# Early flag, unit matrix, output bias and last norms on VectorE, weight preparation in pieces, and a new step order in a four-layer graph kernel

## What is computed

```python
x = _layernorm(x + _L0_gnn_ref(x, adj, W, a))      # attention, one head, leaky ReLU
x = _layernorm(x + _L1_gnn_ref(x, adj, ...))       # attention with logits h A h^T, ELU
x = _layernorm(x + _L2_gnn_ref(x, adj, ...))       # 4 heads; relu(out @ Wo + bo)
x = _layernorm(x + _L3_gnn_ref(x, nodemask, adj, ...))
# L3: one gated sum per relation 2..40, and a "loop" relation 1;
# adj holds only 0 and 1 in these inputs, so only relation 1 contributes
```

## Time and profile before

| | us |
|---|---|
| median of 3 runs | 519.46 (518.91 to 519.73) |
| the profiled execution | 518.74 |
| its span, first to last instruction | 516.9 |
| granted TensorE clock, mean | 0.984 of full speed |
| busy: PE, DVE, ACT, POOL | 478.7, 397.7, 425.1, 317.7 |

### The profile page before, as it was taken

One profiled execution on the slowest core, in us unless ns is written; L12 is line 12 of the kernel. 1 busy time (PEld: TensorE's weight loads), 2 busy tenths in 40 slices (PEclk: granted clock), 3 DMA queues, 4 the chain that ended last, 5 costly groups with the idle time before them and its releaser, 6 DMA issues. The chain is left out here.

```text
span 516.9 us, 14050 instructions
## 1 busy us (share of the span) xinstructions
PE 478.7 (93%) x3964; PEld 411.4 (80%) x3964; DVE 397.7 (77%) x1558; ACT 425.1 (82%) x1261; POOL 317.7 (61%) x717
## 2 busy tenths in 40 slices
PE   3767899999999999999999999999999999999880
PEld 2556788888888898888888888888888888888660
DVE  3486788889888888889888888888987888766540
ACT  2444999989988888999898888898998988898740
POOL 3054456566766766666666676766676676664562
PEclk9988999999999999999999999999999999999996
DMA  6121101122122211222122221122212200000111
GB/s 188 30 83 41 42 13 53 53 63 61 55 63 62 62 44 37 58 63 63 52 64 62 63 58 31 49 63 62 63 52 64 62 23 22 22 22 22 32 32 30
DMA packets 40220, 26.92 MB, mean 52 GB/s; under 512 B 2641, under 2 KB 39889, under 8 KB 40146
## 3 DMA queue, kind: packets, MB, share of 16 engines
q1 hardware_dynamic: 40146, 26.03, 17.4%
HBM read 17.63 MB, written 8.39 MB: 50 GB/s over the span
## 5 line engine op out<-in xcount | busy, mean ns | idle before, releaser
L744 ACT ACTIVATE p<-p,nmax 128x256 f32<-128x256 f32 x256 | 126.6, 498 | 0.4 <-DVE nmax L941 0.4
L1140 POOL TENSOR_SCALAR x<-y,minus_mean,rstd 128x128 f32<-128x128 f32 x256 | 114.7, 458 | 17.7 <-issue 15.9
L1122 POOL TENSOR_TENSOR rstd<-ve,minus_half 128x2 f32<-128x2 f32 x128 | 101.9, 796 | 0.0
L941 DVE CUSTOM_DVE_ANT_0 p<-ps,neg 128x256 f32<-128x256 f32 x256 | 92.7, 419 | 6.6 <-PE ps L520 6.6
L1115 POOL TENSOR_SCALAR ve<-stats 128x2 f32<-128x2 f32 x128 | 24.7, 193 | 110.8 <-DVE stats L854 105.6
L753 ACT COPY p2T<-ps 128x512 f32<-128x512 f32 x128 | 75.0, 595 | 0.0
L531 PE MATMUL ps<-ident,p 128*128 128x128 f32 x512 | 71.7, 273 | 1.5 <-ACT p L744 1.5
L531 PEld LDWEIGHTS ps<-ident,p 128*128 128x128 f32 x512 | 57.4, 141 | 3.2 <-DVE nmax L941 1.4
L977 DVE SCALAR_TENSOR_TENSOR y<-ps,x 128x256 f32<-128x256 f32 x32 | 13.7, 427 | 56.6 <-PE ps L576 56.6
L854 DVE BATCH_NORM_STATS2 stats<-y 128x6 f32<-128x256 f32 x128 | 53.2, 415 | 2.3
L662 ACT COPY xT<-ps 128x256 f32<-128x256 f32 x96 | 36.6, 382 | 17.6 <-PE ps L400 17.1
(11 more groups left out here) (134 smaller groups left out, 1232.3 us busy)
## 6 DMA issues: line engine op xcount, KB each, us to landing
adj_in<-in_adj_dram SPq DMA_DIRECT2D x32, 256.0 KB, 3.0
xT<-in_xT_dram SPq DMA_DIRECT2D x32, 128.0 KB, 2.8
x_in<-in_x_dram SPq DMA_DIRECT2D x32, 128.0 KB, 3.0
x_aside<-x SPq DMA_DIRECT2D x32, 128.0 KB, 2.2
out_dram<-x SPq DMA_DIRECT2D x32, 128.0 KB, 1.8
l_w<-in_l_w_dram SPq DMA_DIRECT2D x1, 257.0 KB
l_w<-in_l_w_dram SPq DMA_DIRECT2D x1, 256.0 KB
first_w<-in_first_w_dram SPq DMA_DIRECT2D x1, 129.0 KB, 2.2
```

Of the source, the lines that this page charges most:

```text
L744: last = nc.scalar.activation(p2(n)[:, k, a, :], p2(n)[:, k, a, :], ACT.Exp, bias=nmax2(n)[:, k, a:a + 1], scale=-1.0, accum_out=sum2(n)[: ...
L941: last = nc.vector.tensor_tensor_reduce(p2(n)[:, k, a, :], bank("sc2", n, a)[:, k * N:(k + 1) * N], neg2(n)[:, k, :], -1.0, HIGHEST, ALU.a ...
L1122: nc.gpsimd.tensor_tensor(rstd[layer](n), ve[layer](n), minus_half[:, :], ALU.pow)\
L1140: last = nc.gpsimd.tensor_scalar(dst[:, k, 0:D], y_t[layer](n)[:, k, :], minus_mean[layer](n)[:, k:k + 1], rstd[layer](n)[:, k:k + 1], ALU ...
```

## The change

- *Flag.* `flag_a` (DVE) takes the maximum and compares it as soon as the last graph's adjacency has been read; `flag`, a 1x1 matmul on PE, counts the partitions over the limit; `flag_b` (DVE) writes the flag. All three run within the last graph's rounds. POOL's all-reduce is gone.
- *Unit matrix.* DVE builds a row index by memsets and four doublings, PE spreads it over the partitions, DVE compares. `lift` comes from it on DVE, `not_eye` on POOL.
- *Output bias.* The matmuls of ones by bias parts and their splitting are gone. `y2` becomes `y2a` (add the bias row) and `y2b` (ReLU and residual) on DVE.
- *Last norms.* For the last three graphs the norms of layers 2 and 3 run on DVE (`end_norm`) and not on POOL.
- *Weight preparation* becomes four steps on PE (`prep_a` to `prep_d`) and four on ACT, placed in the order between other steps; the memsets it needs move from DVE to POOL. `load` becomes four steps on SP (`ld_adj`, `ld_xT`, `ld_x`, `ld_w`), and the weights are loaded ahead of graph 0's x and graph 1's adjacency.
- *Order.* All places in `PLAN` are new. The adjacency ring grows from 3 to 5, the ring `eq1` shrinks from 8 to 7; the mask step is split (`masks`, `neg1`).

The diff, cut to its core; the table of places is shown by one line of each:

```diff
...
-    "gpsimd": [("neg2", 2516), ("var0", 3047), ("rsq0", 3076), ("norm0", 3161), ("var1", 5308), ("rsq1", 5402),
...
+    "gpsimd": [("var0", 11489), ("rsq0", 11689), ("norm0", 11702), ("neg2", 11713), ("var1", 13385), ("rsq1", 13398),
...
-    "adj": 3, "x": 3, "xT0": 2, "neg0": 3, "neg1": 3, "neg2": 6, "eq1": 8, "xw0": 3, "s2row": 2, "p0": 2, "p0T": 2,
+    "adj": 5, "x": 3, "xT0": 2, "neg0": 3, "neg1": 3, "neg2": 6, "eq1": 7, "xw0": 3, "s2row": 2, "p0": 2, "p0T": 2,
...
+AT_END = 3
+GRAPHS = {
+    **{step: (0, 1) for step in ("ld_w", "prep_a", "prep_b", "prep_c", "prep_d",
+                                 "c_prep_a", "c_prep_b", "c_prep_c", "c_prep_d")},
+    **{step: (-1, 0) for step in ("flag_a", "flag", "flag_b")},
+    **{step: (0, -AT_END) for step in ("norm2", "norm3")},
+    **{step: (-AT_END, 0) for step in ("end_norm2", "end_norm3")},
+}
...
 def program(engine, graphs):
 
     return [(name, n) for _, _, name, n in
             sorted((place + 1000 * n, k, name, n)
-                   for k, (name, place) in enumerate(PLAN[engine]) for n in range(graphs))]
+                   for k, (name, place) in enumerate(PLAN[engine]) for n in graphs_of(name, graphs))]
...
+            def ld_adj(n):
                 if n >= RING["adj"]:
                     sp.wait_ge(sem("masks_ready"), n - RING["adj"] + 1)
                     sp.wait_ge(sem("eq1_ready"), n - RING["adj"] + 1)
+                    sp.wait_ge(sem("neg1_ready"), n - RING["adj"] + 1)
                 sp.dma_start(adj_in(n), adj_v[n]).then_inc(sem(f"adj_loaded{n % RING['adj']}"), 16)
+
+            def ld_xT(n):
                 free(sp, "xT0", n, "wh_ps")
                 sp.dma_start(xT0(n), t["xT"][n]).then_inc(sem(f"xT_loaded{n % RING['xT0']}"), 16)
+
+            def ld_x(n):
                 free(sp, "x", n, "y0_ready")
                 sp.dma_start(x_in(n), x_v[n]).then_inc(sem(f"x_loaded{n % RING['x']}"), 16)
-                if n == WEIGHTS_AFTER:
-                    sp.wait_ge(sem("dve_setup"), 2)
-                    for dst, src in weight_loads:
-                        sp.dma_start(dst, src).then_inc(sem("weights_loaded"), 16)
+
+            def ld_w(n):
+                sp.wait_ge(sem("rows_zeroed"), 1)
+                for dst, src in weight_loads:
+                    sp.dma_start(dst, src).then_inc(sem("weights_loaded"), 16)
...
+                pe.wait_ge(sem("index_step"), 5)
+                pe.matmul(ps[:, 3, 0:P], index[0:1, :], ones_row[:, :], start=True, stop=True)\
+                    .then_inc(sem("setup_pe"), 1)
...
-            def setup_later():
+            def prep_a(n):
+                pe.wait_ge(sem("weights_ready"), 1)
                 pe.wait_ge(sem("consts_ready"), 2)
-                pe.wait_ge(sem("lift_ready"), 1)
                 pe.wait_ge(sem("weights_loaded"), WEIGHTS_LOADED)
-                pe.wait_ge(sem("weights_ready"), 1)
...
+            def prep_b(n):
...
+            def prep_c(n):
+                pe.wait_ge(sem("prep_sb"), 1)
...
+            def prep_d(n):
+                pe.wait_ge(sem("prep_sb"), 2)
...
+            def flag(n):
+                o = bank("flag", n)
+                bank_free(pe, "flag", n)
+                pe.wait_ge(sem("excess_ready"), 2)
+                pe.matmul(o[0:1, 0:1], excess[:, :], xw0_all[:, 0, 0, D + 2:D + 3], start=True, stop=True)\
+                    .then_inc(sem("excess_ps"), 1)
...
-                if n == 0:
-                    setup_later()
...
-                    pe.matmul(o[:, k * D:(k + 1) * D], onT(n)[:, k * P:(k + 1) * P], l2_w[:, WO],
-                              start=True, stop=False)
-                    last = pe.matmul(o[:, k * D:(k + 1) * D], ones_bf[:, :], bo_parts[:, :],
-                                     start=False, stop=True)
+                    last = pe.matmul(o[:, k * D:(k + 1) * D], onT(n)[:, k * P:(k + 1) * P], l2_w[:, WO],
+                                     start=True, stop=True)
...
+                for k in range(8):
+                    last = nc.vector.memset(index[:, k:k + 1], float(k))
+                last.then_inc(sem("index_step"), 1)
+                nc.vector.memset(ones_row[:, :], 1.0)
+                for k, size in enumerate((8, 16, 32, 64)):
+                    dve.wait_ge(sem("index_step"), k + 1)
+                    last = nc.vector.tensor_scalar(index[:, size:2 * size], index[:, 0:size], float(size), None, ALU.add)
+                    last.then_inc(sem("index_step"), 1)
...
+                dve.wait_ge(sem("setup_pe"), 1)
+                nc.vector.tensor_tensor(ident[:, :], index[:, :], ps[:, 3, 0:P], ALU.is_equal)\
+                    .then_inc(sem("consts_ready"), 1)
...
-            def setup_biases():
...
-                done(nc.vector.tensor_copy(low[0], bo_row[:, :]), "split_step", 1)
-                done(nc.vector.tensor_tensor(rest[:, 0, :], bo_row[:, :], low[0], ALU.subtract), "split_step", 2)
-                done(nc.vector.tensor_copy(low[1], rest[:, 0, :]), "split_step", 3)
...
+            def y2a(n):
                 dve.wait_ge(sem("wo_ps"), n + 1)
                 free(dve, "y", n, "x3_ready")
                 o = bank("wo2", n)[:, 0:T * D].rearrange("p (t d) -> p t d", t=T)
-                nc.vector.scalar_tensor_tensor(out=y_t[2](n), in0=o, scalar=0.0, in1=x2(n)[:, :, 0:D], op0=ALU.max, op1=ALU.add)\
-                    .then_inc(sem("y2_ready"), 1)
+                nc.vector.tensor_tensor(y_t[2](n), o, bo_row[:, :].rearrange("p (t d) -> p t d", t=1)
+                                        .to_broadcast([P, T, D]), ALU.add).then_inc(sem("y2a_ready"), 1)
+
+            def y2b(n):
...
+                nc.vector.scalar_tensor_tensor(out=y_t[2](n), in0=y_t[2](n), scalar=0.0, in1=x2(n)[:, :, 0:D],
+                                               op0=ALU.max, op1=ALU.add).then_inc(sem("y2_ready"), 1)
+
+            def end_norm(layer, n):
...
+                if n == B - AT_END:
+                    dve.wait_ge(sem(f"x{layer + 1}_ready"), n)
+                for k in range(T):
+                    last = nc.vector.tensor_scalar(dst[:, k, 0:D], y_t[layer](n)[:, k, :],
+                                                   minus_mean[layer](n)[:, k:k + 1], rstd[layer](n)[:, k:k + 1],
+                                                   ALU.add, ALU.mult)
+                last.then_inc(sem(f"x{layer + 1}_ready"), 1)
...
+            def flag_a(n):
+
+                dve.wait_ge(sem("eq1_ready"), B)
+                nc.vector.tensor_reduce(excess_max[:, :], excess_col[:, :], AX.X, ALU.max)\
+                    .then_inc(sem("excess_ready"), 1)
+                dve.wait_ge(sem("excess_ready"), 1)
+                nc.vector.tensor_scalar(excess[:, :], excess_max[:, :], 1.0, None, ALU.is_gt)\
+                    .then_inc(sem("excess_ready"), 1)
+
+            def flag_b(n):
+                dve.wait_ge(sem("excess_ps"), 1)
+                nc.vector.tensor_scalar(excess_flag[:, :], bank("flag", n)[0:1, 0:1], 0.5, None, ALU.is_gt)\
+                    .then_inc(sem("flag_ready"), 1)
...
+                nc.gpsimd.memset(ax_row[:, :], 0.0)
+                nc.gpsimd.memset(last_row[:, :], 0.0)
+                nc.gpsimd.memset(bias_rows[:, :], 0.0).then_inc(sem("rows_zeroed"), 1)
+                nc.gpsimd.memset(minus_half[:, :], -0.5)
                 nc.gpsimd.memset(not_eye[:, :, :], 1.0).then_inc(sem("pool_setup"), 1)
+                pool.wait_ge(sem("rows_zeroed"), 1)
+                nc.gpsimd.memset(last_row[0:1, P - 1:P], 1.0).then_inc(sem("rows_zeroed"), 1)
...
-                nc.gpsimd.affine_select(out=ident[:, :], in_=ident[:, :], compare_op=ALU.not_equal, fill=1.0,
...
+                pool.wait_ge(sem("consts_ready"), 1)
+                for k in range(T):
+                    last = nc.gpsimd.tensor_scalar(not_eye[:, k, k * P:(k + 1) * P], ident[:, :], -1.0, 1.0,
+                                                   ALU.mult, ALU.add)
...
-            pool.wait_ge(sem("excess_ready"), 1)
-            nc.gpsimd.partition_all_reduce(excess_all[:, :], excess_max[:, :], P, bass.bass_isa.ReduceOp.max)\
-                .then_inc(sem("excess_all_ready"), 1)
...
```

156 lines of the change are left out of this document (73 added, 83 removed), and 30 rows, old and new, of the table PLAN.

## The result

The changed kernel took **502.42 us** (median of four runs, 501.53 to 503.85), the kernel before beside it 519.60 (518.91 to 520.16). The ratio is 0.9673, with a 95% interval of 0.9646 to 0.9699. The forecast was 499.2: the direction and the range held, the gain was 17.2 us where the forecast's terms add up to 20.25. The profiled execution took 502.73 for a span of 500.9, against 518.74 for 516.9: 16.0 less.

A forecast was written before the change was run, and what follows sets the result against it. TensorE was taken to bound the middle at 14.43 us a round. End -4.75, output bias -5.4, start -11 and drain +0.9 take 518.74 to 498.5 profiled, plus 0.7 is 499.2 us; range 493 to 508, to hold 8 in 10.

The forecast's parts named there:

- The end: Behind the last norm: with no all-reduce for the flag, only the last store is waited for; 4.75 us less.
- The start: Up to xT2 of graph 0: three things leave the path; 11 us less, bounds 7.5 and 13.5.
- point (1): At the start: unit matrix built on DVE instead of a late GpSimd; the row of s2 starts 3.1 us earlier.
- Point (2): At the start: exp0 of graph 0 no longer waits for ScalarE's weight preparation; 9.1 us earlier, with the earlier unit matrix.
- point (3): At the start: splitting the bias on DVE no longer stands in front of s0; 2.5 us.
- The middle: Full rounds: a timetable shows no late TensorE step, a round of 14.26 us and thin slack of 0.2.
- The drain: Last rounds: a longer wait and added steps, partly given back by norms and wo2; 0.9 us more, bounds 0 and 2.5.
- (a): Middle: the slack is missing, 0.3 us of wait in each of 28 rounds, 8.4 in all; 507.6 us, chance 0.16.
- (d): Middle: h1 comes late and DVE becomes the bound by 0.98 us a round; 526 us, chance 0.05.
- (e): End: the flag still comes last, queued behind DVE's last norms; 499.2 us plus at most 1, chance 0.01.
- (b): Start: prep_b runs wholly uncovered, graph 0 gains 5 us instead of 11; 505 us, chance 0.10.
- (c): Start gains 13.5 us or more, or TensorE has no cold stretches, drain free; 495 us and below, chance 0.08.

The follow-up runs named there:

- e12_flag_alone: Kernel before with the flag alone changed: no GpSimd all-reduce, a matmul sums the flags, unit matrix still on GpSimd; 511.85 us, ratio 0.9854.
- e9_ident_pool: Changed kernel with the unit matrix alone undone: GpSimd writes it by memset and affine select again; 501.87 us, ratio 0.9659.
- e2_prep_once: Changed kernel with the weight preparation in one block behind s2_rows of graph 0 again, its copies behind c_s2; 509.16 us.
- e8_bias_alone: Kernel before with the output bias alone changed: added by a second DVE operation, no bias passes or splitting; 512.50 us, ratio 0.9873.
- e6_neg1_early: Changed kernel with one DVE step moved: the mask neg1 ahead of eq1 instead of behind it; 499.24 us, ratio 0.9637.
- e1_bank: Changed kernel with pT2b1 of the last three graphs taking its bank from PSUM ring b instead of a; 501.38 us, ratio 0.9644.
- e10_drain2: e6_neg1_early with the drain's order changed for graphs 30 and 31 alone, including pT2b1's bank and copy and an earlier flag; 498.86 us, ratio 0.9609.
- e4_flag_end: Changed kernel with the flag undone: reduced behind the last norm, combined by GpSimd's all-reduce and read at the very end; 504.93 us.

## Why the prediction was right, and where not

**The end** held (-4.94 for -4.75): the store is last, and `e12_flag_alone` has the same 3.4 behind the last norm. Against its undoing in the new kernel the flag is worth 2.5 in the median and 4.0 at the end in the profile: 0.9 less than in the old one, since GpSimd is free sooner there. The rest of the difference is the clock of the start.

**The output bias** held in the round: 14.26 alone, with no wait there for DVE's second operation. For all rounds it gave 4.5, the lower bound, where 5.4 was taken.

**The start** came to -10.66 for -11, but point (1) had the wrong cause. The forecast moved the unit matrix off a late GpSimd and kept GpSimd late. The runs show GpSimd late only with the all-reduce in the program; `e9_ident_pool` gives the matrix back to GpSimd for nothing, and `e12_flag_alone`, which leaves the matrix on GpSimd, has the select at 1.85. So what point (1) forecast came from the flag's change, and that the start's sum held is in this part luck. The profile before held a hint that I passed over: the row at 9.05 names "issue", no releaser, and so does the wait of 5.78 at the end. Point (2), ScalarE standing in the preparation, is the large one: 6.7 us by `e2_prep_once`. Of point (3) `e8_bias_alone` found 1.65 at xT1, with a GpSimd that started 0.45 later than before.

**The middle** held: 14.22 and no wait of TensorE between 70 and 422. That the whole stretch came to -4.52 for -4.6 is in part luck. The wait taken as 2 in front of xT2 of graph 31 is 0.26 (466.98), but small waits, three of them for DVE's maxima, bring the last rounds to 2.23 of idle TensorE against 0.93 before, more than the 0.8 taken, and the bias alone gave less than its 5.4. The timetable's slack was not 0.2: 0.75 of added DVE work a round left the round alone. It did miss that neg1 and neg2 would meet.

**The drain** is the mis-sized term: +0.1 forecast from sc2 of graph 31 on, bounds of the whole 0 and 2.5, measured +4.12. The step that failed is "From sc2 (485.33) on all is one chain", with 0.4 for "v2 and pT2b1 behind them". The timetable was laid out for full rounds, where 3.8 us of TensorE work lie between sc2 and pT2b1 of the graph before (262.03 to 265.84 in the kernel after). In the last graph all of it but v2 is missing, and pT2b1 and agg2 of graph 30 come due while graph 31's maxima and exponentials are under way. From sc2 to agg2 of graph 31 the forecast had 0.88 more (0.48 + 0.4); at full clock it is 2.70 more (`e6_neg1_early`), so 1.8 was missed. The bank and the queue of the copy are shown as waits (2.30, then 2.36 in `e1_bank`), but taking both away recovered about 0.55 in all (`e10_drain2`, to wo2 of graph 31), so which part of the order costs the rest stays open. Behind agg2 the forecast held: it had 0.75 less, and at full clock it is 0.84 less (13.00 for 13.84). The remainder is the clock, for which the forecast took nothing: 1.33 behind the new gap and 0.93 behind agg2, nearly all on the last agg3. 2.70 + 1.33 + 0.93 - 0.84 is the measured 4.12.

**The norms**' price held on the row (0.60 a pair for 0.89; from the end of the root to the end of the norm 0.69 for 1.06, so 0.37 a pair where 0.45 was taken), but not their worth: undoing them in the new order costs 1.8 at like clock, where 0.9 was taken, since the norm of graph 31 then stands behind other steps in GpSimd's order. The rule weighed in the prediction, GPSIMD Engine Reference of the Trainium skill, section Engine selection, would have given no difference; the rows speak against it here (0.60 against 0.89).

**Rivals.** (a), (d) and (e) did not happen. Neither did (b) or (c), though in the profile of `e6_neg1_early` the clock alone moves xT2 of graph 0 by 2.2 towards (c).

## What to carry to other kernels

A software pipeline's order has to be laid out for its last graphs as well as for a full round: go through each step that lags by a graph, and ask for its bank and for its copy what is left in between once the next graphs are missing. When an engine idles with no releaser at a program's start, look for what else in the program could cause it before moving its work. And where TensorE's waits are short, what the clock loses behind them has to be counted too: behind the wait of 2.30 it was 1.33 here. When a step is moved to shorten one distance, measure to the next point that both orders share: the 1.86 gained in front of agg2 was 0.55 at wo2.

## What was not expected of the hardware

- GpSimd idles 7.43 to 7.88 us behind its first memsets in the programs with a partition all-reduce (before, `e4_flag_end`, `e8_bias_alone`), and not in those without (0.23 and 0.25 ahead of the same affine select in `e12_flag_alone` and `e9_ident_pool`). Ahead of the all-reduce itself it idles 5.9 to 6.0 again. The Trainium skill, GPSIMD Engine Reference, section Instruction dispatch, gives about 6 us for loading a kernel's code at its first call "with no visible profile instruction". The end agrees with it; the idle at the start, far from any call of the all-reduce, it does not tell of, and what GpSimd does in it no run shows.
- DVE's mask of 128x512 takes 1.41 instead of 0.42 when it starts 0.03 behind a GpSimd operation of 1.15, and GpSimd's pair of norms 1.40 (at 269.34 in the kernel after) instead of 0.89 under DVE work.
- The same code met different clocks: 28 to 32 ran at 0.57 in the kernel after and at 1.00 in `e4_flag_end`, whose program differs in the start by the all-reduce's idle alone. One kernel's runs differ by 0.7 to 5 us, and their mean clocks go with it (`e1_bank`: 496.3 at 0.997, 501.0 at 0.985). That the same gap lowers the clock in some of them and not in others is argued from this, since each kernel has one profile. Which runs get it stays open.
